# Bias additions of the second attention moved into the projection stage, and a matrix split moved between two band selects

## The reference

```
x = x + attn1(layernorm(x), ctx_1024)          # second attention
  qh = q @ Wq.T + bq;  kh = k @ Wk.T + bk;  vh = v @ Wv.T + bv     # 16 heads of 16
  scores = qh . kh / 4, and -inf where |query - key| > 128
  out = softmax(scores) @ vh
  return out @ Wo.T + bo
x = x + ffn1(layernorm(x))                     # gate_w, up_w, down_w: 3 x 8 matrices
```

## Time and profile before

| | us |
|---|---|
| median of 3 runs (lowest, highest) | 1123.39 (1122.06, 1123.60) |
| the profiled execution | 1122.06 |
| its span | 1120.3 |
| TensorE matmuls busy | 1035.5 (92%) |
| VectorE busy | 773.2 (69%) |
| ScalarE busy | 691.0 (62%) |
| GpSimd busy | 563.6 (50%) |
| granted TensorE clock, mean | 0.963 |

### The profile page before, as it was taken

One profiled execution on the slowest core, in us unless ns is written; L12 is line 12 of the kernel. 1 busy time (PEld: TensorE's weight loads), 2 busy tenths in 40 slices (PEclk: granted clock), 3 DMA queues, 4 the chain that ended last, 5 costly groups with the idle time before them and its releaser, 6 DMA issues. The chain is left out here.

```text
span 1120.3 us, 29110 instructions
## 1 busy us (share of the span) xinstructions
PE 1035.5 (92%) x10375; PEld 758.9 (68%) x10376; DVE 773.2 (69%) x2175; ACT 691.0 (62%) x1297; POOL 563.6 (50%) x685
## 2 busy tenths in 40 slices
PE   6999999999999999995689999899999849999995
PEld 3666777777777777774368886455555437888885
DVE  5887887788778887887853316787778774555552
ACT  5888877687668876776454417476767624334331
POOL 4678653556646654311167850496767522323312
PEclk9999999999999999996699999999999968999998
DMA  7633333343353333324856735634444321212201
GB/s 256 178 86 86 87 76 72 72 96 77 73 99 83 90 76 79 76 49 147 272 171 206 209 71 188 192 110 143 142 127 142 114 68 30 34 29 30 30 10 11
DMA packets 124382, 117.25 MB, mean 105 GB/s; under 512 B 47840, under 2 KB 104416, under 8 KB 124128
## 3 DMA queue, kind: packets, MB, share of 16 engines
q1 hardware_dynamic: 116960, 106.32, 34.1%
q0 software_dynamic: 7296, 9.25, 4.9%
HBM read 59.89 MB, written 21.82 MB: 73 GB/s over the span
## 5 line engine op out<-in xcount | busy, mean ns | idle before, releaser
L810 DVE TENSOR_TENSOR e_t_lo<-et,e_t_hi 128x512 f16<-128x512 f32 x256 | 176.7, 690 | 45.7 <-ACT e_t_hi L697 43.7
L704 ACT ACTIVATE e<-masked,neg_max 128x512 f32<-128x512 f32 x256 | 184.4, 720 | 38.2 <-DVE neg_max L836 35.6
L836 DVE CUSTOM_DVE_ANT_0 masked<-sc,mask_bias 128x512 f32<-128x512 f32 x256 | 175.5, 686 | 30.8 <-issue 26.3
L697 ACT ACTIVATE e_t_hi<-et 128x512 f16<-128x512 f32 x256 | 151.4, 591 | 70.8 <-PE et L581 69.4
L581 PEld LDWEIGHTS et<-ident,e 128*128 128x128 f32 x1024 | 124.5, 140 | 56.6 <-issue 8.7
L581 PE MATMUL et<-ident,e 128*128 128x128 f32 x1024 | 154.4, 273 | 1.0 <-ACT e L704 0.8
L74 PE MATMUL ob<-v_hi,e_t_hi 128*128 128x65 f16 x1024 | 119.0, 193 | 1.2 <-issue 1.2
L75 PE MATMUL ob<-v_lo,e_t_hi 128*128 128x65 f16 x1024 | 119.2, 193 | 0.0
L76 PE MATMUL ob<-v_hi,e_t_lo 128*128 128x65 f16 x1024 | 118.4, 193 | 0.0
L2307 ACT ACTIVATE d_e<-d_st 128x384 f32<-128x384 f32 (+1 forms) x192 | 93.4, 528 | 35.9 <-PE d_st L2451 31.8
L74 PE MATMUL h_hb<-h_xt_hi,experts_hi 128*128 128x256 f16 x352 | 97.3, 276 | 2.1 <-DVE h_xt_lo L2684 1.5
(11 more groups left out here) (504 smaller groups left out, 2834.4 us busy)
## 6 DMA issues: line engine op xcount, KB each, us to landing
kk<-nat_k SPq DMA_DIRECT2D x64, 256.0 KB, 3.5
raw<-in_fc SPq DMA_DIRECT2D x16, 1024.0 KB, 7.9
qq<-nat_q SPq DMA_DIRECT2D x64, 128.0 KB, 2.6
qk<-scratch_stack SPq DMA_DIRECT2D x64, 128.0 KB
scratch_stack<-kq_hi SPq DMA_DIRECT2D x16, 256.0 KB, 2.9
scratch_stack<-kq_lo SPq DMA_DIRECT2D x16, 256.0 KB, 3.1
d_expert_raw<-in_gate_w SPq DMA_DIRECT2D x8, 512.0 KB, 3.8
d_expert_raw<-in_up_w SPq DMA_DIRECT2D x8, 512.0 KB, 3.8
```

What stands on the lines that cost most here:

```text
L697: nc.scalar.activation(e_t[u % NBUF].hi[:], et[u % 2][:], ACT.Copy).then_inc(turned_hi, 1)
L704: nc.scalar.activation(e[u % NBUF][:], masked[u % NBUF][:], ACT.Exp, bias=neg_max[:, g % 2, j:j + 1], scale=-1.0).then_inc(exp_ok, 1)
L810: nc.vector.tensor_tensor(e_t[u % NBUF].lo[:], et[u % 2][:], e_t[u % NBUF].hi[:], ALU.subtract).then_inc(turned_lo, 1)
L836: nc.vector.tensor_tensor_reduce(masked[u % NBUF][:], sc[j % 2][:], mask_bias[g // PAIRS % 2][:, j % QT, :], -SCALE0, 3e38, ALU.add, ALU.m ...
```

## The change

It does three things.

- The two bias rows are loaded in `Project1`, right behind the loads of x and ahead of the key stacks, into the place of the first layer's second expert bias (`bias2`), after GpSimd's last use of it (`wb2_ok`). `Project1` gets a GpSimd part that does all twelve additions there: value pieces 0 to 5, x batch 0, value piece 6, x batches 1 and 2, value piece 7, x batch 3, each once ScalarE has copied the piece, or once both engines have normalised the batch.
- In attention 1 the loads, the additions and the wait of matrix 2 for them are gone, and the two small router loads go ahead of the first two matrices.
- GpSimd's subtraction for matrix j stands between the two halves of the band selects of pair j + 5; it stood behind both.

```diff
--- before.py
+++ after.py
@@ -1317,7 +1317,7 @@
 
 class Project1:
 
-    def __init__(self, nc, sem, sb, T, dram, pb, tb):
+    def __init__(self, nc, sem, sb, T, dram, pb, tb, bias, bias_free):
         stats, mv = sb("c_stats", [P, NT, 6]), sb("c_mv", [P, NT, 2])
         sd, rstd, shift = (sb(n, [P, B, QT]) for n in ("c_sd", "c_rstd", "c_shift"))
         warm = sb("c_warm", [P, 1])
@@ -1327,6 +1327,7 @@
         names = ("var_ok", "sd_ok", "rstd_ok", "shift_ok", "z_act", "z_dve", "turned", "z_copied", "proj", "v_copied", "q_hi", "q_lo", "v")
         (var_ok, sd_ok, rstd_ok, shift_ok, z_act, z_dve, turned, z_copied, proj, v_copied, q_hi, q_lo, v) = (sem("c" + n) for n in names)
         x_in = [sem(f"cx_in{b}") for b in range(B)]
+        bv, bo, bias_in = bias[:, 0, :], bias[:, 1, :], sem("cbias_in")
         bank_free = [sem(f"cbank_free{i}") for i in range(JOB_BANKS)]
 
         def bank(job):
@@ -1336,6 +1337,9 @@
             sp.wait_ge(T.rows_added, EXPERTS0 * ADDED)
             for b in range(B):
                 sp.dma_start(T.x[:, b * QT:(b + 1) * QT, :], dram["acc"][b * S:(b + 1) * S, :].rearrange("(t p) d -> p t d", p=P)).then_inc(x_in[b], 16)
+            sp.wait_ge(bias_free, EXPERTS0)
+            for dst, name in ((bv, "bv1"), (bo, "bo1")):
+                sp.dma_start(dst, dram[name].unsqueeze(0).to_broadcast([P, D])).then_inc(bias_in, 16)
             for n in range(KEYS_FIRST, B * DT):
                 sp.wait_ge(T.keys_lo, n + 1)
                 stack_rows(sp, dram, kq[n], 1, n, T.keys_stacked)
@@ -1347,6 +1351,28 @@
                     sp.wait_ge(T.ones_set, 3 * QBUF)
                     for pair in range(EARLY_LOADS):
                         load_stacks(sp, T, dram, pair)
+
+        def gpsimd(pool):
+            def add_value_bias(n):
+                pool.wait_ge(v_copied, n + 1)
+                part = T.v1[:, 2 * n:2 * n + 2, :, 0:DH]
+                pool.tensor_tensor(part, part, bv.rearrange("p (h d) -> p h d", d=DH).unsqueeze(1).to_broadcast([P, 2, HEADS, DH]), ALU.add).then_inc(T.v_ready, 1)
+
+            def add_output_bias(b):
+                tiles = slice(b * QT, (b + 1) * QT)
+                pool.wait_ge(z_act, 2 * (b + 1))
+                pool.wait_ge(z_dve, 2 * (b + 1))
+                pool.tensor_tensor(T.x[:, tiles, :], T.x[:, tiles, :], bo.unsqueeze(1).to_broadcast([P, QT, D]), ALU.add).then_inc(T.bo_added, 1)
+
+            pool.wait_ge(bias_in, 32)
+            for n in range(6):
+                add_value_bias(n)
+            add_output_bias(0)
+            add_value_bias(6)
+            add_output_bias(1)
+            add_output_bias(2)
+            add_value_bias(7)
+            add_output_bias(3)
 
         def scalar(act):
             def values(n):
@@ -1519,7 +1545,7 @@
             batch_queries(2)
             batch_queries(3)
 
-        self.sync, self.scalar, self.vector, self.tensor = sync, scalar, vector, tensor
+        self.sync, self.gpsimd, self.scalar, self.vector, self.tensor = sync, gpsimd, scalar, vector, tensor
 
 
 def phase_experts0(nc, sem, T, W, dram):
@@ -1546,7 +1572,8 @@
             sem("f" + n) for n in ("turned", "affine", "h_full", "h_act", "fc2_done", "weight_ok", "wb2_ok", "res_ok"))
         added = T.rows_added
         E = EXPERTS0
-        project = Project1(nc, sem, sb, T, dram, [kb[0][:], kb[1][:]] + [bank[:].rearrange("p c n -> p (c n)") for bank in tb], [hb, ob_half])
+        project = Project1(nc, sem, sb, T, dram, [kb[0][:], kb[1][:]] + [bank[:].rearrange("p c n -> p (c n)") for bank in tb], [hb, ob_half],
+                           W.bias2, wb2_ok)
         GATHERED = 16 * HALVES
 
         with nc.Block() as block:
@@ -1632,6 +1659,7 @@
                     if e >= 1:
                         scatter(e - 1, range(HALVES))
                 scatter(E - 1, range(HALVES))
+                project.gpsimd(pool)
 
             @block.scalar
             def _(act):
@@ -2196,15 +2224,15 @@
         o_t = [Split(sb, f"d_o_t{i}", [P, 2, DT, P]) for i in range(2)]
         expert_raw = [sb(f"d_expert_raw{i}", [P, MATRIX]) for i in range(RAWS1)]
         e = [sb(f"d_e{i}", [P, 2, BLOCKS, P]) for i in range(EBUF)]
-        bv, bo = expert_raw[2][:, 0:D], expert_raw[2][:, D:2 * D]
         expert_raw_in = [sem(f"dexpert_raw_in{i}") for i in range(RAWS1)]
         expert_hi, expert_lo = sem("dexpert_hi"), sem("dexpert_lo")
         wk = [ps(f"d_wk{i}", [P, 512]) for i in range(WORKS)]
         st = [ps(f"d_st{i}", [P, 512]) for i in range(3)]
         ob, tr = ps("d_ob", [P, S]), ps("d_tr", [P, QT, 4, ROWS4])
-        names = ("bias_in", "v_ready", "bo_added", "banded", "work_full", "work_free", "max_ok", "shift_hi", "shift_ok", "st_full", "exp_ok",
+        names = ("banded", "work_full", "work_free", "max_ok", "shift_hi", "shift_ok", "st_full", "exp_ok",
                  "pv_done", "heads_ok", "heads_turned", "rden_ok", "normed", "o_t_hi")
-        (bias_in, v_ready, bo_added, banded, work_full, work_free, max_ok, shift_hi, shift_ok, st_full, exp_ok,
+        v_ready, bo_added = T.v_ready, T.bo_added
+        (banded, work_full, work_free, max_ok, shift_hi, shift_ok, st_full, exp_ok,
          pv_done, heads_ok, heads_turned, rden_ok, normed, o_t_hi) = (sem("d" + n) for n in names)
         finish_turned, finish_hi, finish_lo, finish_full = (sem("dfinish_" + n) for n in ("turned", "hi", "lo", "full"))
         route = Route1(nc, sem, sb, T, dram, out, expert_raw, e, st, wk, tr[:].rearrange("p a b c -> p (a b c)"), pv_done, exp_ok, expert_lo)
@@ -2224,11 +2252,9 @@
                         sp.wait_ge(st_full, PARTS * (n - QBUF + 1))
                     load_stacks(sp, T, dram, n)
 
-                for dst, name in ((bv, "bv1"), (bo, "bo1")):
-                    sp.dma_start(dst, dram[name].unsqueeze(0).to_broadcast([P, D])).then_inc(bias_in, 16)
+                route.load(sp)
                 for j in range(2):
                     load_matrix(sp, dram, expert_raw, expert_raw_in, j)
-                route.load(sp)
                 for n in range(PAIRS1):
                     sp.wait_ge(shift_ok, n + 1)
                     for w in range(2):
@@ -2239,10 +2265,7 @@
                         stack_rows(sp, dram, T.kq[n + LATE_QUERIES], 0, n + LATE_QUERIES, T.q_stacked[(n + LATE_QUERIES) // DT])
                     j = n + 2 - SPLIT_AT
                     if 2 <= j < MATRICES:
-                        if j == 2:
-                            sp.wait_ge(v_ready, NT // 2)
-                            sp.wait_ge(bo_added, B)
-                        else:
+                        if j > 2:
                             sp.wait_ge(expert_lo, j - 2)
                         load_matrix(sp, dram, expert_raw, expert_raw_in, j)
                 for old in spent:
@@ -2251,15 +2274,6 @@
 
             @block.gpsimd
             def _(pool):
-                pool.wait_ge(bias_in, 32)
-                def add_value_bias(n):
-                    part = T.v1[:, 2 * n:2 * n + 2, :, 0:DH]
-                    pool.tensor_tensor(part, part, bv.rearrange("p (h d) -> p h d", d=DH).unsqueeze(1).to_broadcast([P, 2, HEADS, DH]), ALU.add).then_inc(v_ready, 1)
-
-                def add_output_bias(b):
-                    tiles = slice(b * QT, (b + 1) * QT)
-                    pool.tensor_tensor(T.x[:, tiles, :], T.x[:, tiles, :], bo.unsqueeze(1).to_broadcast([P, QT, D]), ALU.add).then_inc(bo_added, 1)
-
                 def keep_band(n, a):
                     pool.wait_ge(exp_ok, PARTS * n + 3 * a + 3)
                     for first, sign in ((2, 1), (1, -1)):
@@ -2267,20 +2281,16 @@
                         pool.affine_select(out=blocks, in_=blocks, compare_op=ALU.is_ge, fill=0.0, base=0,
                                            pattern=[[0, QT - 1], [sign, P]], channel_multiplier=-sign).then_inc(banded, 1)
 
-                for n in range(NT // 2):
-                    add_value_bias(n)
                 for slot in range(SLOTS1):
                     if 0 <= slot - 2 < PAIRS1:
                         keep_band(slot - 2, 0)
-                    if 0 <= slot - 2 < PAIRS1:
-                        keep_band(slot - 2, 1)
-                    if 0 <= slot - 4 < B:
-                        add_output_bias(slot - 4)
                     j = slot - SPLIT_AT
                     if 0 <= j < MATRICES:
                         cols = slice(j * MATRIX, (j + 1) * MATRIX)
                         pool.wait_ge(expert_hi, j + 1)
                         pool.tensor_tensor(T.experts1.lo[:, cols], expert_raw[j % RAWS1][:], T.experts1.hi[:, cols], ALU.subtract).then_inc(expert_lo, 1)
+                    if 0 <= slot - 2 < PAIRS1:
+                        keep_band(slot - 2, 1)
                 route.gpsimd(pool)
 
             @block.scalar
@@ -2827,6 +2837,7 @@
                 T.q_stacked = [sem(f"q_stacked{b}") for b in range(B)]
                 T.loaded = [sem(f"loaded{i}") for i in range(QBUF)]
                 T.ones_set = sem("ones_set")
```

(1 more changed line is left out.)

## The result

| | before | after |
|---|---|---|
| median us (lowest, highest; runs) | 1122.72 (1121.6, 1123.6; 4) | 1138.15 (1137.84, 1138.6; 4) |
| profiled execution, its span | 1122.06, 1120.3 | 1138.74, 1137.0 |
| granted clock, mean | 0.963 | 0.961 |
| VectorE busy, GpSimd busy | 773.2, 563.6 | 783.1, 565.8 |

The ratio of the two kernels' times is 1.0138 [1.012, 1.0155], with its 95% interval in brackets: 15.4 us slower, where I had forecast 10.6. The time lies above the predicted range.

What follows compares the result with a forecast made beforehand. TensorE, busy for most of the span, was taken to bound the kernel, waiting at attends for GpSimd's last selects. Terms 10.1 - 0.3 + 0.8 = 10.6 us gave 1134.0 us from the runs' median; range 1127 to 1137.

Steps and rivals of the forecast that it cites:

- The subtraction between the halves: Attention 1: the last band selects, and so attends 2 to 13, start 0.84 us later each, 10.1 in all.
- The bias additions leave attention 1: Start of attention 1: without the value additions the selects end sooner and the gap before attend 0 goes, -0.3 us.
- The additions go into the projection stage: Projection stage: GpSimd, idle there, does 18.6 us of additions and ends near 703.0, before VectorE's last instruction; cost 0.
- The rule weighed: Projection stage: additions would hold up VectorE's normalisations if in a two-port mode; 408 ns spoke against it, left out of sum.
- More than forecast: Projection stage rival: rows land with the key stacks, or additions block normalisations by up to 2.36; +2.4, 1136.4 us; chance 0.10.
- The cover: End of projection stage: VectorE's last instruction, ending at 704.6, hides GpSimd's additions, which end at about 703.0.
- The row loads: Projection stage: two row loads ahead of the key stacks on SP delay ScalarE's query copies, +0.8 us.
- Half absorbed: Attention 1 rival: the slot after a late attend is shorter by half the delay, main term 5, 1129 us; chance 0.12.
- not slower: Attention 1 rival: earlier subtraction frees matrix buffers sooner, shorter ScalarE waits pay the 10.6; 1122 to 1124 us; chance 0.10.

Runs made afterwards that it cites:

- x7: Kernel before, with GpSimd's subtraction between the band halves in even slots only, odd pairs keeping it behind: 1122.64 us, 0.9997.
- x9: Kernel before, with the subtraction cut into two of 512 columns, one between the band halves and one behind them: 1123.55 us, 1.0003.
- x1: Kernel before with only the reordering (subtraction between the band halves), bias additions staying in attention 1: 1133.5 us, 1.0089.
- x2: Kernel after with only the reordering taken back, so bias loads and additions stay in the projection stage: 1128.53 us, 1.0046.
- x11: x2 with GpSimd adding a constant 0 (one-operand tensor_scalar) in place of the bias row: 1127.43 us, 1.004.
- x5b: Kernel before with the two row loads and sixteen GpSimd memsets in the projection stage, additions staying in attention 1: 1123.72 us, 1.0000.

## Why the prediction was wrong

- *The subtraction between the halves, 12 x 0.84 = 10.1.* Right in mechanism and size. The trace gives 0.86 before each of the twelve attends, plain cycles of 11.2, and 9.6 more idle time; alone it costs 10.0, with the additions still in its way. x7 and x9 show its two conditions, odd pairs only and only what outlasts the sixth exponential.
- *The bias additions leave attention 1, -0.3.* The trace has it (from the first matmul to attend 0, 18.43 became 18.12), but kernels with the additions in place showed 18.1 to 19.8. Not shown. What the additions' leaving did save, 2.5 at attends 2 and 3 as x1 has it, is counted nowhere in the forecast, since in the old order they cost next to nothing there (x2: 0.1).
- *The additions go into the projection stage: cost 0.* This is the step that failed. The forecast measured GpSimd's work against the moment at which the barrier waits for it, and took for granted that the work costs nobody else anything. It cost VectorE 8.9 us, nearly all on the path: +8.35 in the trace of the kernel after; alone, in x2, 7.45 in the trace and 5.2 in the executions.
- *The rule weighed and left out.* I took 408 ns for 256 columns, as long as the statistics, as a sign that `c_z` runs in no mode that shares a port with GpSimd. It runs 0.41 alone and 2.43 beside an addition, so the duration alone was no sign of it. The Trainium skill, "SBUF — State Buffer", section "Who interferes with whom", has GpSimd and a tensor_scalar in a two-port mode exclude each other for a whole instruction, and a VectorE instruction with two SBUF inputs wait only for a GpSimd one that reads. No row names the mode of `c_z`. Beside additions and memsets the rows agree in both: `c_z` waited for either, `c_shift` (two inputs) for additions only, `c_stats` (one input) and `kq_lo` (one of its inputs in PSUM) for none. Beside GpSimd's one-operand form in x11 they don't: `c_z` waited 0.38 at most, not a whole instruction of 1.48.
- *The size of that rival.* "More than forecast" named it, but with one wait of 2.36. Each of the `c_z`, `c_sd` and `c_shift` of three batches can meet an addition, 12 instructions, and in the trace 9 of them did. Counted so, at half to one mean addition (18.6 / 12 = 1.55) each, my estimate for the rival would have been 9 to 19 us, and 7 to 14 with the 9.
- *The cover.* 703.0 against 704.6 was the wrong comparison too. GpSimd's end counts 2.99 us before attention 1 and VectorE's 0.44, so its cover ended at 702.06 and the forecast 703.0 would have cost 0.9. After, it costs nothing, since the late VectorE covers it (705.53 + 2.99 is well ahead of 713.39).
- *The row loads, +0.8.* 0.5 in the trace, nothing in the time.
- *Half absorbed, and not slower.* Both are refuted: the plain cycles stayed at 11.2 one behind the other. Of the 0.9 between 10.1 and the 9.2 of the trace, 0.3 is the earlier attend 0. The other 0.6 lie at attends that were late already: attend 7 (0.40), whose cycle grew from 10.86 to 11.21 only, attend 12 (10.52 to 11.22) and attend 14 (12.59 to 12.49). ScalarE's waits for matrices over 740 to 885 us stayed about the same (19.6 before and 19.3 after).

## What to carry to other kernels

An idle engine is free only if its instructions don't hold up the one that is on the path. Before moving additions to GpSimd, list the tensor_scalars from SBUF to SBUF and the instructions with two SBUF inputs that VectorE executes in that window, and price each at up to one GpSimd addition; statistics and the instructions that read PSUM did not wait here. If the work must go there, cut it into short instructions, which took back 5.5 of the 7.5 us that the stage had lost, and 3.1 of 5.2 in the time. Work placed between two steps of a chain is free up to the moment when the next step's input arrives and costs in full beyond it; and where GpSimd works up to a barrier, count the 3 us that pass behind it.

## What the runs showed of the hardware

- VectorE's tensor_scalar from SBUF to SBUF waits for the end of a GpSimd addition of two tiles or a memset, however little it moves itself (128x4: 0.17 alone, 1.06 beside additions of 1.17), with scalars from a tile or constants. Beside GpSimd's tensor_scalar (1.48) it waited 0.38 at most.
- VectorE's scalar_tensor_tensor with two inputs in SBUF waited for additions (128x4: 0.16 alone, up to 1.80) and not for memsets (0.161 to 0.164); statistics from SBUF (0.41) and a scalar_tensor_tensor with an input in PSUM (0.74) did not wait for additions.
- GpSimd was hardly slowed by the same meetings: a value addition took 1.17 (6.99 / 6) beside VectorE and 1.14 (9.15 / 8) in attention 1.
- A GpSimd addition of 128x512 in place of two of 128x256 is 1.17 against 1.33 us: cutting costs 14% of GpSimd's time. An addition of 128x1024 in four such pieces is 2.78 and not 2.36, 18%.
- From GpSimd's last instruction to the next stage's first matmul pass 2.99 to 3.00 us (five kernels), whatever its length; from VectorE's, where it ends last, mostly 0.44 (once 0.75, in x5b). What fills the 3 us is not shown.
